# Graph network on one core: one gather per tile into fixed slots, and a last stage shared between GpSimd and ScalarE

## The reference

```python
def _L0(h, src, dst, W1, b1, W2, b2, eps):          # 3 layers
    for l in range(3):
        agg = segment_sum(h[src], dst, n)
        h = maximum(((1 + eps[l]) * h + agg) @ W1[l] + b1[l], 0) @ W2[l] + b2[l]
    return h

def _L1(h, w, a, src, dst):                         # attention over edges
    hi, hj = h[src], h[dst]
    exp_e = exp(leaky_relu(concatenate([hi, hj], -1) @ w, 0.2) @ a)
    att = exp_e / segment_sum(exp_e, src, N)[src]
    return segment_sum(hi * att, dst, N)

x = layernorm(x + _L0(x, ...)); x = layernorm(x + _L1(x, ...))
```

## Time and profile before

| | us |
|---|---|
| median of 3 runs (12926.82 to 12962.32) | 12931.7 |
| the profiled execution | 12954.3 |
| its span | 12952.3 |
| PE busy, share of the span | 6629.0, 51% |
| POOL busy | 7452.4, 58% |
| DVE busy | 5013.5, 39% |
| ACT busy | 682.1, 5% |

### The profile page before, as it was taken

The page is one execution under the profiler, slowest core; times in us unless marked ns, Lnnn a source line. Parts: engine busy times, 40 slices in busy tenths (PEclk is TensorE's granted clock), DMA queues, the critical chain, the costliest instruction groups (busy, mean ns, idle before and its releaser), DMA issues.

```text
span 12952.3 us, 200391 instructions
## 1 busy us (share of the span) xinstructions
PE 6629.0 (51%) x29626; PEld 5438.9 (42%) x29627; DVE 5013.5 (39%) x20694; ACT 682.1 (5%) x1668; POOL 7452.4 (58%) x8006
## 2 busy tenths in 40 slices
PE   3333343343333433443344344566676677777776
PEld 2233233332333333333233333455666666666665
DVE  2222222232222222232222222455555555666666
ACT  0000000000000000000000000111111111100001
POOL 4555555545555555545555555455555555588886
PEclk6555555555555555555555555677777777777776
DMA  2111111111111111121111111254444444433333
GB/s 70 38 39 38 38 38 38 38 51 39 39 39 38 39 38 39 37 56 38 38 39 39 38 39 38 79 136 131 129 129 127 127 126 125 117 99 97 95 96 94
DMA packets 889258, 883.54 MB, mean 68 GB/s; under 512 B 241058, under 2 KB 707128, under 8 KB 889187
## 3 DMA queue, kind: packets, MB, share of 16 engines
q0 software_dynamic: 225904, 515.07, 15.2%
q1 hardware_dynamic: 597889, 251.76, 7.0%
q10 hardware_dynamic: 65426, 116.27, 3.2%
HBM read 743.81 MB, written 137.14 MB: 68 GB/s over the span
## 4 chain that ended last, share of the span: by engine, by line
issue 45%; PE 38%; DVE 6%; SPq 4%; DVEq 2%; another core or an unknown queue 2%; POOL 1%; DMA 1%; ACT 1%; POOLq 0%; ACTq 0%
PE psum L933 18%; PE psum L1062 6%; PE psum L1035 5%; PE psum L1032 4%; PE psum L1017 4%; DVE agg L1226 3%; PE psum L1050 2%; SPq L489 2%; DVEq L1226 1%; POOL hot L688 1%; SPq L558 1%; DVE hot L1215 1%; PE psum L944 0%; DVEq L378 0%
## 5 line engine op out<-in xcount | busy, mean ns | idle before, releaser
L933 PE MATMUL psum<-rows,hot 128*128 x9984 | 3170.2, 479 | 4930.6 <-issue 4014.8
L933 PEld LDWEIGHTS psum<-rows,hot 128*128 128x128 f32 x9984 | 2475.6, 308 | 5625.3 <-issue 5521.7
L642 POOL DMA_INDIRECT rows<-table_g,idx_now x3126 | 3026.6, 968 | 2454.9 <-SPq L483 1376.8
L1226 DVE TENSOR_TENSOR agg<-agg,psum 128x128 f32 x6656 | 1913.7, 288 | 6337.4 <-PE psum L933 4181.7
L642 POOL DMA_INDIRECT rows<-table_p,idx_now x1563 | 1517.7, 971 | 1321.2 <-SPq L483 873.9
L642 POOL DMA_INDIRECT rows<-in_x,idx_now x1563 | 1507.7, 965 | 1204.9 <-SPq L483 755.2
L688 POOL TENSOR_SCALAR hot<-iota_f,big 128x128 f32<-128x128 f32 x1664 | 1327.7, 810 | 325.1 <-DVE big L1434 273.0
L1035 PE MATMUL psum<-rows,ident 128*128 x3328 | 946.7, 377 | 535.2 <-issue 473.2
L1062 PE MATMUL psum<-rows,hot 128*128 x3328 | 918.4, 406 | 359.3 <-SPq L568 251.2
L1032 PE MATMUL psum<-big,work 128*128 x3328 | 916.9, 368 | 279.4 <-issue 242.2
L1035 PEld LDWEIGHTS psum<-rows,ident 128*128 128x128 f32 x3328 | 706.8, 263 | 660.6 <-issue 644.4
(11 more groups left out here) (147 smaller groups left out, 2333.3 us busy)
## 6 DMA issues: line engine op xcount, KB each, us to landing
x_of<-rows SPq DMA_DIRECT2D x390, 256.0 KB
rows<-x_of SPq DMA_DIRECT2D x390, 256.0 KB, 3.3
work<-rel_rows ACTq DMA_DIRECT2D x208, 256.0 KB
big<-lo_rows ACTq DMA_DIRECT2D x208, 256.0 KB, 3.8
rows<-table_g,idx_now POOLq DMA_INDIRECT x3126
rows<-in_x,idx_now POOLq DMA_INDIRECT x1563
rows<-table_p,idx_now POOLq DMA_INDIRECT x1563
idx_now<-src_r SPq DMA_DIRECT2D x784, 4.0 KB
```

Source lines behind the costliest of these rows:

```text
L642: pool.indirect_dma_start(out=slots[:, j, 0:wide], out_offset=None, in_=table, in_offset=bass.IndirectOffsetOnAxis(ap=idx_now[:, j:j + 1], ...
L933: pe.matmul(ps[j][:, 0:D], hot[:, j, :], rows_of(tiles[j], D), start=True, stop=True).then_inc(rows_used, 1)
L1226: dve.tensor_tensor(to, to, sums, ALU.add).then_inc(bank_free, 1)
```

## The change

1. Every tile gets its own gather: 1664 per stage in place of 1563. Tile t always lies in slot t mod 16, so the slot's address and the waiting value are known without a number from memory. `src_r` (indices by row) goes, and `src_t` (by tile) is made before the first layer, no longer between the first and the second. It costs 13 more gathers of indices ahead of layer 1, which stood behind layer 1 before.
2. TensorE waits on `row_in[t]`, the gather's own semaphore. `arrived`, SP's relay and `need_row` go. In the layers SP waits for the half's use and then stages the next indices; `free` stays in the score stage alone.
3. `sum_tiles` loops over turns of 16 tiles; DVE and, in the score stage, TensorE load only the windows (`tile_win`).
4. Last stage: ACT makes one-hots 0, 2, 3, 5, 6 of each 8 (Abs of the distance, then Relu of weight minus weight times distance), POOL 1, 4, 7. The look-up on TensorE and DVE serves tiles 0 to 5; for tiles 6 and 7 POOL gathers the reciprocals from a table in HBM, `table_r`, asked for two halves ahead. DVE writes the negated weights and destinations beside the others and the two columns of indices. `x1_of` is reloaded per 4 tiles instead of per 8.
5. In the score stage ACT writes the exponential a second time, negated.

```diff
-            def gather_half(no, turn, h, table, wide, n):
+            def gather_half(no, turn, h, table, wide):
-                pool.wait_ge(staged[h], 16 * (no * (FULL + 1) + turn + 1))
-                pool.wait_ge(free, no * HALVES + 2 * turn + h + 1)
+                pool.wait_ge(staged[h], gathers(no, turn))
+                if no == LAYER_A:
+                    pool.wait_ge(free, 2 * turn + h + 1)
                 stand_alone(pool)
-                for j in range(h * HALF, h * HALF + n):
+                for j in range(h * HALF, (h + 1) * HALF):
                     pool.indirect_dma_start(out=slots[:, j, 0:wide], out_offset=None, in_=table,
...
+            def stage_rest(no):
+                with sp.Fori(0, TURNS - 1) as i:
                     for h in range(2):
+                        sp.wait_ge(rows_used, USED + no * T + i * TPI + (h + 1) * HALF)
                         stage_half(h, 2 * i + h + 2)
...
             def sum_tiles(no, done, hots, hot0, per_hot):
-                with pe.Fori(0, GROUPS) as g:
-                    tiles = load_tiles(g * HALF, PE_E)
-                    for j in range(HALF):
-                        pe.wait_ge(bank_free, done + g * HALF + j + 1)
-                        if j % per_hot == 0:
-                            pe.wait_ge(hots, hot0 + g * (HALF // per_hot) + j // per_hot + 1)
-                        wait_row(no, tiles[j])
-                        pe.matmul(ps[j][:, 0:D], hot[:, j, :], rows_of(tiles[j], D), start=True, stop=True).then_inc(rows_used, 1)
+                with pe.Fori(0, TURNS) as i:
+                    for t in range(TPI):
+                        pe.wait_ge(bank_free, done + i * TPI + t + 1)
+                        if t % per_hot == 0:
+                            pe.wait_ge(hots, hot0 + i * (TPI // per_hot) + t // per_hot + 1)
+                        pe.wait_ge(row_in[t], gathers(no, i))
+                        pe.matmul(ps[t % HALF][:, 0:D], hot[:, t % HALF, :], row_of(t, D), start=True, stop=True).then_inc(rows_used, 1)
...
             def weigh_half(turn, h):
                 pool.wait_ge(weight_ready, 2 * turn + h + 1)
-                pool.wait_ge(rel_kept, 2 * turn + h + 1)
-                for j in range(HALF):
+                for j in HOT_POOL:
...
+            def fetch_half(group, h):
+                pool.wait_ge(idx_ready, group + 1)
+                for k, j in enumerate(FETCHED):
+                    pool.indirect_dma_start(out=rden_e[:, h * HALF + j:h * HALF + j + 1], out_offset=None, in_=table_r, ...)
...
+                def distance(n):
+                    act.wait_ge(hot_act, len(HOT_ACT) * (group + 2) + max(n - 1, 0))
+                    act.activation(away[:, n % 2, :], iota_f[:, :], ACT.Abs, bias=rel_neg[:, t:t + 1]).then_inc(away_ready, 1)
+                def weigh(n):
+                    act.wait_ge(away_ready, len(HOT_ACT) * group + n + 1)
+                    act.wait_ge(rows_used, LAYER_B * T + turn * TPI + t + 1)
+                    act.activation(hot[:, j, :], away[:, n % 2, :], ACT.Relu, bias=weight[:, t:t + 1],
+                                   scale=weight_neg[:, t:t + 1]).then_inc(hot_act, 1)
...
-                dve.wait_ge(hot_w_ready, HALF * (group + 1))
-                dve.tensor_tensor(weight[:, s * HALF:(s + 1) * HALF], rden_e[:, s * HALF:(s + 1) * HALF],
-                                  exp_t[:, ds(TPI + group * HALF, HALF)], ALU.mult).then_inc(weight_ready, 1)
+                for k in range(FETCHES):
+                    dve.wait_ge(rden_in[s * FETCHES + k], 16 * (lap + 1))
+                dve.tensor_copy(rel_2[:, :, here], rel_both[:, :, ds(group * HALF, HALF)])
+                dve.tensor_tensor(weight_2[:, :, here], rden_e[...], exp_both[...], ALU.mult).then_inc(weight_ready, 1)
+                if more:
+                    dve.tensor_copy(idx_now[:, s * FETCHES:(s + 1) * FETCHES], src_t[:, ds(first, FETCHES)]).then_inc(idx_ready, 1)
```

More of the change, by code:

```diff
@@ L51 @@
 ROW = PW + D
-WINDOW = 2048
 NEG_SLOPE = 0.2
@@ L59 @@
 LAYER_A, LAYER_B = LAYERS, LAYERS + 1
+LOOKED = (0, 1, 2, 3, 4, 5)
+FETCHED = (6, 7)
+HOT_POOL = (1, 4, 7)
+HOT_ACT = (0, 2, 3, 5, 6)
+LOOKS = len(LOOKED)
+LO_HOTS = 2
+FETCHES = len(FETCHED)
+assert LOOKED + FETCHED == tuple(range(HALF))
 assert EP * EC == E and QROWS >= T and PP * PC == QPAD - E
-assert HALF < LEFT < TPI and QROWS == T
+assert QROWS == T
 class Count:
@@ L374, in stand_alone, with load_windows @@
             eng.sem_inc(passed, 1)
-        def load_tiles(first, engine):
+        def load_windows(first, engine):
             _, values = nc.values_load_multi_w_load_instructions(
-                tile_row[0:1, ds(first, HALF)], engines=(engine,), min_val=0, max_val=(WINS - 1) * WINDOW + T - WINS,
-                skip_runtime_bounds_check_because="a tile's window and row, by their making")
+                tile_win[0:1, ds(first, HALF)], engines=(engine,), min_val=0, max_val=WINS - 1,
+                skip_runtime_bounds_check_because="a tile's window, by its making")
             return list(values)
[L383 to L387, removed]
-        def slot_of(tile):
-            return tile & (TPI - 1)
         def n_chunks(b):
@@ L423, in x_parts, with gathers @@
             return 2 if b == LAST else 1
[L425 to L428 removed]
+        def gathers(no, turn):
+            return 16 * (no * TURNS + turn + 1)
         def flip(eng, bank, rows_in, n):
@@ L796, in exponentials @@
                 act.wait_ge(exp_ready, i + 1)
+                act.activation(exp_both[:, 1, ds(i * TPI, TPI)], exp_now[:, :], ACT.Copy, scale=-1.0)
                 act.activation(exp_t[:, ds(i * TPI, TPI)], exp_now[:, :], ACT.Copy).then_inc(exp_kept, 1)
@@ L1030, in _ @@
                             sums = ps[j % BANKS][:, k * PW:(k + 1) * PW]
-                            tile = tiles[t - h * HALF]
                             pe.matmul(sums, hot_t[:, t // QUAD, (t % QUAD) * P:(t % QUAD + 1) * P],
-                                      q_rows[:, ds(window_of(tile) * PW, PW)], start=True, stop=False)
-                            wait_row(LAYER_A, tile)
-                            pe.matmul(sums, ident[:, :], rows_of(tile, PW),
+                                      q_rows[:, ds(windows[t - h * HALF] * PW, PW)], start=True, stop=False)
+                            pe.wait_ge(row_in[t], gathers(LAYER_A, i))
+                            pe.matmul(sums, ident[:, :], row_of(t, PW),
                                       start=False, stop=True).then_inc(rows_used, 1)
@@ L1054, in sum_half @@
                 group = 2 * turn + h
-                tiles = load_tiles(group * HALF, PE_E)
                 for j in range(HALF):
@@ L1207, in _ @@
             take_edges(1, rel_t)
-            dve.wait_ge(info_in, 32)
+            own.add(dve.tensor_single_scalar(g_lo, g_src, P - 1, ALU.bitwise_and))
+            own.wait()
+            dve.tensor_copy(g_lo16, g_lo).then_inc(g_ready, 1)
+            dve.wait_ge(info_in, 16)
             dve.wait_ge(g_taken, 2 * QUADS)
```

309 lines of the change are left out of this document (154 added, 155 removed).

## The result

| | before | after |
|---|---|---|
| median | 12934.1 us | 12219.9 us |
| ratio (95% interval) | | 0.9445 (0.9429 to 0.9461) |
| the profiled execution | 12954.3 | 12219.6 |

The change saves 714 us. I forecast 1,324 less (11,610, range 10,700 to 12,500): the direction was right and the time is in the range, but the saving is little more than half of the forecast. The experiments then showed something larger: on two of the four chips that they ran on, the traces show no crawl, the kernel before takes 9,912 to 9,926 us there, and every version with 1664 gathers that ran there is 3.7 to 4.6% slower than it. The changed kernel itself wasn't run on such a chip. The first runs were of the crawling kind.

A forecast was written before the change was run, and what follows sets the result against it. Gathers were taken to slow TensorE's sequencer, so slots are freed late and gathers stop. Layers -911, score stage -332, last stage -66, preparation -14 sum to -1323 from 12954.3: 11631, median 11,610 us, range 10,700 to 12,500.

The forecast's parts named there:

- crawl: TensorE's register instructions, layers and score stage: about 691 ns each while POOL gathers, 36 ns afterwards; taken as 17 us per burst.
- The turn: Layers, 16 tiles: static slots bring 25.8 us to 22.9 (ends 20.3 and 27.0), 911 us less over 312 turns.
- TensorE's L936 and L938 at about 0.7 us during bursts: Layers: a sign that the forecast is right, TensorE's sequencer instructions staying slow while POOL gathers.
- POOL's wait behind index copies of under 250 us a layer: Layers: a sign that the forecast is right, POOL's idle time behind index copies falling below 250 us a layer.
- The index copy: Layers: the copy now stands behind the wait for use; 1.7 us added per turn, all 4.3 at the upper end.
- The score stage: Half of 8 tiles falls from 13.6 to 12.0 us with fewer TensorE sequencer instructions: -332 us (-706 to 0).
- The last stage: Half falls to 7.5 us with fewer VectorE selections and the one-hots split: -66 us (-170 to +163).
- The preparation: Between stages: earlier `src_t` -38, thirteen index gathers +16, reciprocal table and first fetches +8; together -14 us (-30 to +20).
- A: Rival, 20%: POOL becomes the bound everywhere, turn 20.3 us, score half 10.5, about 10,490 us in all.
- B: Rival, 7%: slower, the crawl covers more of each turn, turn 26.5 us, score half 13.8, about 13,110 us.
- C: Rival, 18%: the last stage is slowed by its own fetches, its half 8.6 us, 11,840 us in all.
- D: Rival, 8%: the crawl isn't paid per instruction, static slots give nothing, layers stay at 25.8 us per turn, about 12,750.

The follow-up runs named there:

- e10: Changed kernel with VectorE using fixed chunks, no windows and one wait per four tiles in the layers, sums left out: 12,143 us, ratio 0.9364 to the kernel before.
- e4: Changed kernel with SP copying a half's indices ahead of their use and POOL itself waiting for the use: 10,385 us against 9,926 for the kernel before.
- e3: Changed kernel with VectorE's loop in the layers handling 16 tiles instead of 8: 10,380 us against 9,926 for the kernel before, ratio 1.046.
- e9: Kernel before with only the last stage's one-hots split between ACT and POOL: 12,973 us against 12,956, ratio 1.0012.
- e7: Changed kernel without the last stage's gathers of reciprocals, all eight tiles looked up: 12,359 us against 12,326 for the changed kernel on that chip.

## Why the prediction was right or wrong

**What bounds the kernel.** "Gathers slow TensorE's sequencer, TensorE frees the slots late, gathers stop" was a true reading of that trace, and fixing TensorE did pay. It was incomplete in two ways. The slow instructions were not TensorE's own trouble: with TensorE relieved, VectorE's line 1228 took 699 ns in the burst shown. And with TensorE ahead, its finished products are counted up to 11 us late (e10, and the changed kernel's own turn above), which taking nearly all of VectorE's instructions away doesn't cure: the layer stays at 2,515 us against 2,539. That slow instructions and late counts have one cause is argued, not shown. In the kernel before, in the turn of the earlier trace rows, the counts weren't late: TensorE's last product there ends at 2073.23, and VectorE's sum follows 0.2 us behind.

```profile
2073.41 0.29 DVE L1226 TENSOR_TENSOR agg<-agg,psum 128x128 f32 x1 [5.30 <-PE psum L933]
```

**The turn, the term that was mis-sized.** I priced a tile at 2.25 x 0.8 = 1.8 us of TensorE in the crawl, and the turn at 22.9. TensorE's instructions in fact ran at full speed (L936 has a median of 32 ns in layer 2), and tiles went at POOL's 1.25 us until the one-hots failed to come. My sign for this, TensorE's L936 and L938 at about 0.7 us during bursts, didn't come, and neither did POOL's wait behind index copies of under 250 us a layer (511.2). The turn then is POOL's own (1607.3 + 486.8) / 104 = 20.1, and its wait for the late use and the copy, (511.2 - 66.5) / 104 = 4.3 without the one ahead of the layer: 24.4. "Where a stall goes, say what is late next" is what the sum missed; the forecast's sum has 1323 us of saving and the profiled executions have 734.7, and 497 of the 588 between them lie here (7642 against 7145).

**The index copy.** I added 1.7 us for it, and POOL's wait now has its name (511.2 us in a layer). But the copy is only the last link: of the 6.85 us at 4020.78 above, 4.42 had passed when the copy was issued at 4018.35. e4 shows it worth nothing without the crawl; with the crawl it wasn't tried.

**The score stage.** 12.75 for 12.0, inside its ends of 10.2 and 13.6. The value was a middle, for want of a row, and 155 us of the 588 are its share. e3, where nothing crawls, takes 10.2 (2126 / 208), which is the lower end.

**The last stage.** 7.2 for 7.5: VectorE isn't the busiest alone, as forecast, but level with TensorE (991.1 and 991.0 us of 1498). Two gathers per half bring no crawl; one of TensorE's lines in 10700 to 12150:

```profile
L1061 PEldq ALU_OP  x603: 32/32/36, 10704.2 to 12148.2; - x151
```

The rule of the Trainium skill ("SBUF — State Buffer", in the warning on DVE blocking DMA) shows no cost at this size: the fetches take 988 ns each beside a VectorE busy 66% of the stage. How much of that time VectorE spent in the mode that the warning is about, no row says. My account of why was off: I gave the gain to fewer selections. The fetches, which save them, are worth 33 us, and the larger part came together with static slots and reload, and with it went TensorE's wait on SP's relay, which I hadn't priced in this stage (e9).

**The preparation.** I had -14. The five stages together save 719 of the 734.7 us, so what lies outside them changed by -16.

**The rivals.** A was right in its mechanism on another chip and wrong in its consequence: where TensorE keeps up, the turn is 20.3 us, as it said, but there the kernel before keeps up as well, by its time, so the extra gathers are a loss. That is a case which I didn't list: slower, because what the change cures is absent. B (the crawl never ends) did not come: the bursts grew to 24 gathers and were still followed by a pause. C is out by e7, and D by TensorE's "issue" time falling from 1337.9 to 169.0. The prediction also cited the Trainium skill, "Runtime: NRT & Kernel Launch", Instruction fetch mechanics, for a sequencer that stalls only at certain taken branches. With the crawl the changed kernel's trace disagrees as the first one did (699 against 40 ns for line 1228, inside and behind a burst); e3's agrees (40 throughout).

## What to carry to other kernels

Before trusting a stall that one trace shows, run the unchanged kernel on more than one chip: here the stall came with some chips only, and the sign of the change's worth hung on it (0.94 with it; without it 1.04, for its nearest versions). When a stage is gated by one engine's work items (here POOL at 1.25 us per gather), a change that adds 6% of them needs the cover of a stall elsewhere, and costs time where the stall isn't there. And when two engines that wait for the same semaphore start within 0.1 us of each other long after the producer ended, suspect the signal, not the waiting engines.

## What the runs showed of the hardware that I had not expected

- Two kinds of chip. The first runs and two groups gave 12,934, 12,956 and 13,137 us for the kernel before, two other groups 9,926 and 9,912. Between the changed kernel and e3, nearly the same code, the difference lies in the stages that gather rows by indirect DMA (a layer takes 2,539 to 2,553 or 2,106 to 2,113 us, the score stage 2,651 or 2,126; the last stage 1,498 or 1,501).
- On the crawling kind, increments made by TensorE during a burst of gathers step the semaphore one per 3 to 5 us in e10's stretch, and the rest together about 4 us behind the burst, while the gathers' own landings still reach TensorE in time for its products to keep the 1.25 us pace.
- Its traces also hold fewer records of semaphores: 65,870 steps in the changed kernel's, 179,114 in e3's. Nearly all that is missing are landings of DMAs (42,009 against 148,903); of the engines' own steps 23,861 and 30,211 are there. Whether the recording has a part in the delay, why chips differ, whether fewer increments would cure the layers on a chip that crawls (theory M), and whether backward branches have a part in it (theory F, tried only without the crawl) stay open.
- ScalarE's two steps took 400 ns (Abs, 128x128, bias by pointer) and 478 ns (Relu, bias and scale by pointer), POOL's gather of 128 single values 988 ns, hardly more than the 966 of 128 rows of 512 bytes.
